# A cross-attention layer and a recurrent layer on one core: work regrouped into two-head units, with new orders for all engines

## The reference

```python
q  = layer_norm((x   + pos_enc).T, ln_q_g,  ln_q_b)        # 256 x 128
kv = layer_norm((ctx + pos_enc).T, ln_kv_g, ln_kv_b)
Q, K, V = split(q @ Wq), split(kv @ Wk), split(kv @ Wv)    # 16 heads of 8
ctx = softmax(Q @ K.T / sqrt(8)) @ V
r   = ctx @ Wo + q
out = gelu(layer_norm(r) @ W1 + b1) @ W2 + b2 + r
x   = out.T                                                # 128 x 256
```

```python
xn = _ln(x); sx = previous row of xn - xn
xxx = tanh((xn + sx * maa_x) @ maa_w1)                     # 5 groups of 32
x5 = xn + sx * (maa_stack + xxx @ maa_w2)                  # 5 mixed inputs
w = exp(-exp(time_decay + tanh(x5[1] @ decay_w1) @ decay_w2))
r, k, v, g = x5[3] @ Wr.T, x5[0] @ Wk.T, x5[2] @ Wv.T, silu(x5[4] @ Wg.T)
for t in range(128):                                       # per head, s is 8 x 8
    a = k_t (outer) v_t;  out_t = r_t @ (u * a + s);  s = a + w_t * s
att = group norm of out over the 8 values of a head
x = x + (att * g) @ Wo.T;  xn2 = _ln(x);  sx2 = previous row - xn2
x = x + sigmoid((xn2 + sx2 * ffn_maa_r) @ Wr.T) * (square(relu((xn2 + sx2 * ffn_maa_k) @ Wk.T)) @ Wv.T)
```

## Time and profile before

| | |
|---|---|
| median of 3 runs | 512.01 us (505.37 to 515.03) |
| span of the profiled execution | 508.9 us; its own time is not given apart, and the runs put it some 3 us above the span |
| PE busy | 393.7 us (77%) |
| DVE busy | 296.2 us (58%) |
| ACT busy | 216.9 us (43%) |
| POOL busy | 149.4 us (29%) |
| mean granted TensorE clock | 0.826 of 2.4 GHz |

### The profile page before, as it was taken

One profiled execution on the slowest core, in us unless ns is written; L12 is line 12 of the kernel. 1 busy time (PEld: TensorE's weight loads), 2 busy tenths in 40 slices (PEclk: granted clock), 3 DMA queues, 4 the chain that ended last, 5 costly groups with the idle time before them and its releaser, 6 DMA issues.

```text
span 508.9 us, 6721 instructions
## 1 busy us (share of the span) xinstructions
PE 393.7 (77%) x2512; PEld 266.0 (52%) x2512; DVE 296.2 (58%) x626; ACT 216.9 (43%) x473; POOL 149.4 (29%) x102
## 2 busy tenths in 40 slices
PE   2437668769887998799989888998997996684624
PEld 0402323526564677367756756675666565563613
DVE  1134144246565967497859776966776455754622
ACT  1201433553564367336735763475446546115001
POOL 4100100110444053415241722263025407235240
PEclk9999999857975899589859986987798689779556
DMA  8340240050314032303421150305030003003000
GB/s 265 144 92 1 64 81 3 20 125 1 95 52 94 6 91 73 83 12 86 117 39 52 44 135 1 95 3 135 1 95 11 2 12 82 11 1 93 10 1 11
DMA packets 35953, 29.74 MB, mean 58 GB/s; under 512 B 3536, under 2 KB 33616, under 8 KB 35792
## 3 DMA queue, kind: packets, MB, share of 16 engines
q1 hardware_dynamic: 35776, 25.86, 20.9%
q10 hardware_dynamic: 144, 3.45, 1.7%
HBM read 20.78 MB, written 8.39 MB: 57 GB/s over the span
## 4 chain that ended last, share of the span: by engine, by line
PE 39%; issue 19%; DVE 15%; POOL 10%; DMA 8%; SPq 4%; ACT 4%; POOLq 0%; ACTq 0%
DMA k_stack<-stacks 6%; POOL v_rep L764 5%; DVE top L808 4%; PE o_bank L363 4%; PE r_one L369 4%; PE h_sum L446 3%; PE r_two L501 3%; PE a_even L412 3%; PE o_bank L550 3%; PE r_one L356 2%; PE r_two L369 2%; PE a_odd L389 2%; PE h_even L434 2%; SPq L308 2%; DVE st L902 2%
## 5 line engine op out<-in xcount | busy, mean ns | idle before, releaser
L808 DVE TENSOR_REDUCE top<-a_even 128x2 f32<-128x512 f32 x64 | 44.1, 688 | 46.9 <-PE a_even L412 33.4
L626 ACT ACTIVATE probs<-h_even 128x512 f32<-128x512 f32 x64 | 38.4, 599 | 57.2 <-PE h_even L434 34.6
L412 PE MATMUL a_even<-k_stack,q_stack 48*128 48x256 bf16 x128 | 32.0, 341 | 31.5 <-DMA k_stack<-stacks 26.8
L771 POOL TENSOR_TENSOR hrs<-hvar,mhalf 128x32 f32<-128x32 f32 x8 | 44.4, 5546 | 37.0 <-DVE hvar L928 37.0
L808 DVE TENSOR_REDUCE top<-a_odd 128x2 f32<-128x512 f32 x64 | 43.6, 682 | 12.9 <-PE a_odd L412 12.9
L902 DVE TENSOR_TENSOR_SCAN st<-dec_rep,v_rep 128x1024 f32<-128x1024 f32 x16 | 40.4, 2528 | 11.6 <-ACT dec_rep L697 5.8
L626 ACT ACTIVATE probs<-h_odd 128x512 f32<-128x512 f32 x64 | 38.6, 603 | 18.5 <-PE h_odd L434 17.7
L446 PE MATMUL h_sum<-probs,v_pad 128*32 128x256 f32 x512 | 43.2, 468 | 0.0
L764 POOL TENSOR_TENSOR v_rep<-v_rep,rk 128x1016 f32<-128x1016 f32 x16 | 39.8, 2485 | 0.0
L434 PE MATMUL h_even<-q_stack,k_stack 50*128 50x256 bf16 x128 | 32.6, 346 | 5.8 <-ACT probs L626 5.3
L412 PEld LDWEIGHTS a_even<-k_stack,q_stack 48*128 48x128 bf16 x128 | 7.7, 101 | 54.1 <-DMA k_stack<-stacks 30.5
(11 more groups left out here) (159 smaller groups left out, 825.2 us busy)
## 6 DMA issues: line engine op xcount, KB each, us to landing
...
W<-in_weights ACTq DMA_DIRECT2D x1, 3368.0 KB, 11.1
stacks<-parts SPq DMA_DIRECT2D x16, 192.0 KB, 2.4
q_stack<-stacks SPq DMA_DIRECT2D x16, 192.0 KB, 3.5
k_stack<-stacks SPq DMA_DIRECT2D x16, 192.0 KB, 4.5
...
```

Of the source, the lines that this page charges most:

```text
L412: mm = pe.matmul(a_score[head % 2][:, j * T:(j + 1) * T], q_stack[g.p][e:e + SCORE_ROWS, head // 2, j * 128:(j + 1) * 128], k_stack[g.p][e ...
L626: act.activation(flat(probs[turn % PROBS][:, :, :]), h_score[HEAD_ORDER[turn] % 2][:, :], ACT.Exp, scale=SCORE_SCALE).then_inc(s_probs, 1)
L771: pool.tensor_tensor(hrs[:, :], hvar[:, :], mhalf[:, :], ALU.pow).then_inc(s_hrs, 1)
L808: dve.tensor_reduce(top[:, :, head], a_score[head % 2][:, :].rearrange("p (a t) -> p a t", a=2), AX.X, ALU.max).then_inc(s_top, 1)
```

## The change

`AT` and `PERIOD` give way to `ORDER`, one written list of operations for each engine (`top.3.5` is part 5 of item 3), no longer periodic. The parts:

- **Two-head units.** `top`, `scores` and `probs` work on a unit of two heads, 8 per item, in one of two PSUM pairs of two banks each (`pairs`), which both kinds share in turn. A reduction or exponential covers 1024 columns.
- **Direct stacks.** The three parts go straight from SBUF into the stacks by 12 DMAs per item, without DRAM.
- **Shared banks.** The other four banks (`banks`) serve all other stretches of all items; `BANKS` says which, and PE waits for the previous user (`wait_bank`).
- **Layer norms in token layout.** `centre` also transposes, so that VectorE adds the centred position code (`dev`), reduces the squares (`ssa`), and multiplies (`nrm`); four transposes (`back`) return it. `var`, `spread`, `h_var`, `h_spread` and POOL's `zsum` go.
- **Mixing.** `maa_stack` becomes a row of the matmul; three products and three sums of up to 512 columns replace L871 and L880, all on VectorE.
- **State.** It is split by value columns, four per scan. Both products by r (`rst`) are on VectorE; `kv` stays on POOL. `read` is 8 matmuls with a constant stationary side of 32 columns and 256 moving columns. The u term is a POOL product (`rkp`), two matmuls and a product (`bon`).
- **Group norm.** Centring moves into a matmul (`cturn`), the squares to ACT, leaving four VectorE operations.
- **First operation of VectorE.** `spread_u` scales a constant of the large weight block and waits for it.

```diff
--- before.py
+++ after.py
...
-        "var_a": 1541, "nrm": 1586, "left": 1645, "parts": 1720,
...
+        "spread_u.0 dev.0 dev.1 var_a.0 var_a.1 nrm.0 dev.2 nrm.1 dev.3 var_a.2 left.0 var_a.3 nrm.2 parts.0 dev.4 var_a.4 "
...
+BANKS = {
+    "dev": "01200030", "nt": "32201011", "qk": "11220111", "v": "33211322", "guard": "10103121", "sum": "30022010",
...
+OPENS = {"centre": "dev", "back": "nt", "qk": "qk", "v": "v", "guard": "guard", "sums.0": "sum", "turn_sums": "sums_t", "turn_ctx": "ctx_t",
...
+        pairs = [stack.enter_context(nc.psum_tensor(f"pair{p}", [128, 4, T], F32)) for p in range(2)]
+        banks = [stack.enter_context(nc.psum_tensor(f"bank{p}", [128, 512], F32)) for p in range(4)]
...
+        def bank(stretch, n):
+            return banks[int(BANKS[stretch][n])]
...
+        def wait_bank(pe, stretch, n):
...
+            if before[stretch, n]:
+                last, m = before[stretch, n]
+                pe.wait_ge(closes[last], m * 3 + thirds[last] if last in thirds else m + 1)
...
-                if a := due(at, "SP", "stack"):
...
-                        sp.wait_ge(s_score_t, (a.n - 1) * H0)
-                    sp.wait_ge(s_spilled[a.p], dma(a, 6))
-                    for side, dst in enumerate((q_stack, k_stack)):
-                        for e in range(2):
-                            sp.dma_start(dst[a.p][64 * e:64 * e + SCORE_ROWS, :, :],
-                                         stacks[a.p, side].rearrange("(i e d) r t -> e (d r) i t", e=2, d=D0)[e]).then_inc(s_stacked[a.p], 16)
...
+                    for side, (tile, which) in enumerate(((q_stack, Q_ROWS), (k_stack, K_ROWS))):
+                        for row in which[part]:
+                            sp.dma_start(tile[p][row::8, :, :], parts[p][:, part, side, :]).then_inc(s_stacked[p], 16)
...
-                if a := due(at, "PE", "var"):
-                    pe.wait_ge(s_dev, a.n * 2 + 2)
-                    for j in range(4):
-                        mm = pe.matmul(a_odd[:, j:j + 1], devsq[:, j // 2, (j % 2) * 128:(j % 2) * 128 + 128], w("mean"),
...
+                p = n % 2
+                if op == "centre":
+                    wait_bank(pe, "dev", n)
+                    pe.wait_ge(s_x_in[p], dma(n, 2))
+                    for side in range(2):
+                        for j in range(2):
+                            mm = pe.matmul(bank("dev", n)[:, (side * 2 + j) * 128:(side * 2 + j + 1) * 128], xin[p][:, side, j * 128:(j + 1) * 128],
+                                           w("center"), start=True, stop=True)
+                    mm.then_inc(s_centred, 1)
+                if op == "back":
...
+                    wait_bank(pe, "nt", n)
...
+                if op == "top":
+                    wait_pair(pe, (op, n, part))
...
                     for j in range(2):
...
+                        for e in range(2):
+                            mm = pe.matmul(pair(op, n, part)[:, 2 * e + j, :], q_stack[p][64 * e:64 * e + TOP_ROWS, part, j * 128:(j + 1) * 128],
+                                           k_stack[p][64 * e:64 * e + TOP_ROWS, part, :], start=True, stop=True)
+                    mm.then_inc(s_scored, 1)
...
-                    if o := due(at, "PE", "read", half):
-                        pe.wait_ge((s_rst_low, s_rst_high)[half], o.n + 1)
-                        for d in range(S1):
-                            mm = pe.matmul(o_bank[:, (half * S1 + d) * 16:(half * S1 + d + 1) * 16], st[:, half, d, :], w("heads"),
-                                           start=True, stop=True)
-                        if half == 1:
-                            mm.then_inc(s_att, 1)
...
+                if op == "read":
+                    wait_bank(pe, "read", n)
+                    pe.wait_ge(s_rst, n * 2 + 2)
+                    for second, name in enumerate(("heads_a", "heads_b")):
+                        for quad in range(4):
+                            mm = pe.matmul(bank("read", n)[quad * QUAD:(quad + 1) * QUAD, 0:E], w(name), flat(st[:, 2 * quad + second, :, :]),
+                                           start=second == 0, stop=second == 1)
+                    mm.then_inc(s_read, 1)
+                if op == "cturn":
...
-                if r := due(at, "POOL", "rst_low"):
-                    pool.wait_ge(s_st, r.n * 2 + 1)
-                    pool.tensor_tensor(st[:, 0, :, :], st[:, 0, :, :], rk[r.p][:, 0, 0, None, :].broadcast_to([128, S1, NT]), ALU.mult).then_inc(s_rst_low, 1)
...
+                if op == "dev":
+                    dve.wait_ge(s_centred, n + 1)
...
+                    dve.tensor_tensor(dev[p][:, :, :, :], bank("dev", n)[:, :].rearrange("p (s j c) -> p s j c", s=2, j=2),
+                                      pe_c[:, None, :, :].broadcast_to([128, 2, 2, 128]), ALU.add).then_inc(s_dev, 1)
+                if op == "var_a":
+                    dve.wait_ge(s_sqa, n + 1)
+                    dve.tensor_reduce(ssa[p][:, :], sqa[:, :, :], AX.X, ALU.add).then_inc(s_ssa, 1)
...
+                if op == "top":
+                    dve.wait_ge(s_scored, n * UNITS + part + 1)
+                    dve.tensor_reduce(top[p][:, :, :, part].rearrange("p j e -> p e j"), pair("top", n, part)[:, :, :].rearrange("p (e j) t -> p e j t", e=2), AX.X, ALU.max).then_inc(s_top, 1)
...
-                        for group in ((0, 1), (2, 3), (4,))[part]:
-                            src = (r_one, r_two, r_one)[part]
-                            for half in range(2):
-                                col = (group % 2) * 256 + half * 128 if group < 4 else half * 128
-                                ins = dve.scalar_tensor_tensor(out=mixed[:, group, half, :], in0=src[:, col:col + 128], scalar=v(f"stack{group}_{half}"),
-                                                               in1=sx[:, half, :], op0=ALU.add, op1=ALU.mult)
...
-                if r := due(at, "DVE", "ruk"):
...
-                        ins = dve.scalar_tensor_tensor(out=ruk[r.p][:, half, :], in0=rk[r.p][:, 0, half, :], scalar=v(f"faaaa_{half}"),
-                                                       in1=rk[r.p][:, 1, half, :], op0=ALU.mult, op1=ALU.mult)
...
+                    dve.tensor_tensor(mixed[p][:, 2 * part:2 * part + count, :, :],
+                                      bank(("m2a", "m2b", "m2c")[part], n)[:, 0:count * E].rearrange("p (k h t) -> p k h t", k=count, h=2),
+                                      sx[p][:, None, :, :].broadcast_to([128, count, 2, NT]), ALU.mult).then_inc(s_mix, 1)
+                if op == "mixed":
+                    dve.wait_ge(s_mix, n * 3 + part + 1)
+                    groups = slice(2 * part, 2 * part + len(MIX_GROUPS[part]))
+                    dve.tensor_tensor(mixed[p][:, groups, :, :], mixed[p][:, groups, :, :],
+                                      xt[p][:, None, :, 1:NT + 1].broadcast_to([128, len(MIX_GROUPS[part]), 2, NT]), ALU.add
+                                      ).then_inc((s_mixed0, s_mixed1, s_mixed2)[part], 1)
...
+                    dve.tensor_tensor_scan(line(st[:, states, :, :]), line(decay[p][:, :, :, :]), line(v_rep[p][:, states, :, :]),
+                                           0.0, ALU.mult, ALU.add).then_inc(s_st, 1)
+                if op == "rst":
+                    dve.wait_ge(s_st, n * 2 + part + 1)
+                    states = slice(4 * part, 4 * part + 4)
+                    dve.tensor_tensor(st[:, states, :, :], st[:, states, :, :], rk[p][:, 0, None, :, :].broadcast_to([128, 4, 2, NT]), ALU.mult
+                                      ).then_inc(s_rst, 1)
...
+                    dve.scalar_tensor_tensor(out=yo[p][:, :], in0=y[:, :], scalar=0.5, in1=x2[p][:, :], op0=ALU.mult, op1=ALU.add).then_inc(s_done, 1)
+                if op == "spread_u":
+                    dve.wait_ge(s_weights, 16)
+                    for half in range(2):
+                        dve.tensor_scalar(spread_u[:, half, :], w("spread"), v(f"faaaa_{half}"), None, ALU.mult).then_inc(s_spread_u, 1)
...
```

1388 lines of the change are left out of this document (734 added, 654 removed), and 88 rows, old and new, of tables (BANKS, ORDER).

## The result

The changed kernel takes **383.44 us** in the median of four runs (381.46 to 384.74), against 512.92 us for the kernel before beside it (four runs, 505.37 to 515.03). The forecast was 373 us, with a range of 338 to 440.

What follows compares the result with a forecast made beforehand. PE, with VectorE next, was taken to set the period, and the two to be level after the change. Start 35, middle 306 and tail 29 gave a 370 us span, 373 us as median; range 338 to 440.

Steps and rivals of the forecast that it cites:

- PE per item: PE's matmul work for one item: from 45.1 to 34.4 us, or 40.2 if pairs save nothing.
- keep their columns: Centring, projections, mixing matmuls and feed-forwards on PE: same columns as before, so a change of 0.
- VectorE per item: VectorE's work for one item: from 37.3 to 35.8 us, including 2.0 us of waiting on GpSimd.
- The alternative beside it: VectorE: by the skill's contention rule, two-SBUF-input operations are exposed and kv blocks fully, total some 27 us higher.
- The start: Up to the first top: VectorE queued behind spread_u's wait for the weight block until 17.4 us; first top at 35.
- The middle: Between first top and tail: PE 253 and VectorE 257 us, level; at 84% full, 306 us.
- from there six items are ready or nearly so: After the first top: VectorE and PE would have work without a gap.
- The tail: From the last read to the end: read 1.9 us, 28.0 following, group norm 0.8 shorter; 29 us.
- Stalls: Fixed lists and shared PSUM banks delay several items: VectorE at 65%, middle 395, total 462 (401 to 502); chance 0.25.
- The list fits well: Engine lists 94% full or more, or VectorE and GpSimd hardly excluding each other: 340 us or less; chance 0.10.
- The lower clock: PE's granted clock stays at 1.2 GHz with less work and more waiting: 527 us in all; chance 0.05.
- The words are not what is done: kv stays on GpSimd; VectorE waiting 4.8 us per item would give 400 us, inside the forecast; no separate chance.

Runs made afterwards that it cites:

- e6: Changed kernel with both heads of each top and scores unit read from the same half of the array's rows; 401.41 us.
- e8: Changed kernel with both kv products and their column copies moved from GpSimd to VectorE, each ahead of its scan; 380.81 us.
- e1: Changed kernel with spread_u moved in VectorE's list from its head to just before item 0's first maximum; 380.56 us.
- e5: Changed kernel with spread_u late and the large weight block issued only after item 0's first exponential; 375.83 us.
- e2: As e1, with the k_stack DMAs of items 0 and 1 issued by ScalarE's queue instead of SP's; 380.53 us.
- e12: Changed kernel with the edits of e5 and e8, plus the k_stack DMAs of items 0 and 1 on ScalarE's queue; 373.22 us.
- e7: Changed kernel with the three mixing sums per item on GpSimd in place of VectorE; 401.1 us.
- e9: Changed kernel with the lower product of the state by r (rst, part 0) on GpSimd, the upper staying on VectorE; 405.05 us.
- e4: Changed kernel with read in its earlier form, sixteen matmuls of 128 by 16 instead of eight of 32 by 256; 413.30 us.

## Why the prediction was right, point by point

- **PE per item**: 34.4 forecast, 36.2 in the run (289.6 / 8). That the middle still agrees to 2 us (253 and 254.6) is partly luck, for two errors cancel: PE's whole work was 289.6 us instead of 275, but 35.0 of it lay in the start and the tail, where 22 was taken off. `read` hit (1.3, 1.27). `top` and `scores` were better than forecast (6.6 for 7.6): the overlap that the prediction took from one pair of the earlier trace rows is real, and worth 36 us of PE (e6). What was dearer is in part the start: centring (L479) takes about 2 us for each of the first four items and 1.1 from 80 us on, as one item had in the period before (L378, 1.1), so the prediction's "keep their columns" holds in the dense stretch and not ahead of it. The rest wasn't traced.
- **VectorE per item**: 35.8 forecast, 36.1 in the run. The 2.0 us carried over for waiting on GpSimd measured 1.9 to 2.3 (e8). It was a choice between 0 and 4.8, so the near hit is partly luck. The alternative beside it, that all instructions with two SBUF inputs are exposed and the sum is 27 us higher, did not come: most of the instructions stretched are these, but only when a product runs at the same time, and that is 1.9 us per item.
- **The start**: 35 forecast, 37.0 came. The step "`spread_u` waits for the weight block, everything on VectorE is queued behind it" was true and incomplete. The same block held PE by way of `xin` (e1, e5): with the first wait gone the first `top` came 2 us earlier, with both gone 8.8. Both waits end at 17.1, so the sum did not suffer.
- **The middle**: 306 forecast at 84%, 316 came at 81%. The step that failed is "from there six items are ready or nearly so, and VectorE and PE have work without a gap". From 37 to 80 us VectorE is 61% busy, afterwards 85%. At 85% these 26.4 us of work would take 31: 12 us lost, the whole difference. The 84% itself was a choice between two rows that lie 17 points apart; that the dense stretch has 85% fits it, but no reading of the old profile gave it, and the hole behind the first maxima was not in it. SP's issues were priced at 0.4 us by a row of another form; the strided ones take 0.6 to 0.65. But a second queue for items 0 and 1 brought nothing (e2, e12), so theirs are not the cause. The rows behind this point show two waits of VectorE that fill the loss, 9.98 us for item 0's transposed sums and 5.41 for the first `top` of item 2. SP's queue issues item 2's stacks only from 63.93, behind `guard.1` in its list, and the last at 71.18. But PE's `top` of item 2 starts at 74.04 without idle time of PE before it, so what held it last was PE's own list, in which it stands behind item 1's scores and sums. With the start 9 us earlier (e5) the two waits were 10.17 and 5.41. That the order of these lists makes them is read, not tested. Timeline of the changed kernel, VectorE:

```profile
68.25 0.36 DVE L1005 RECIPROCAL rden<-bank 128x32 f32<-128x32 f32 x1 [9.98 <-PE bank L551]
...
74.47 2.36 DVE L989 TENSOR_REDUCE top<-pair 128x4 f32<-128x1024 f32 x2 [5.41 <-PE pair L510]
```

PE, and SP's queue:

```profile
74.04 0.90 PE L510 MATMUL pair<-k_stack,q_stack 62*128 62x256 bf16 x8
...
62.37 1.04 SPq L423 DMA_DIRECT2D q_stack<-guard_t  x2
63.93 1.86 SPq L419 DMA_DIRECT2D q_stack<-parts  x3
```

- **The tail**: 29 forecast, 28.4 came, and 28.40 again in e5. The last `read` takes 1.94 us (1.9 forecast), so 26.5 us remain for the rest, where 27.2 was forecast.
- **The rivals.** *Stalls* would have needed 65% in the middle; it had 81. *The list fits well* is not excluded by much: with e5's and e8's edits together the time was 372, still well above 340. *The lower clock* did not come: the mean rose from 0.826 to 0.905. In the stretch from 37 to 80 us it was 0.70, with PE busy for 74% of it. *The words are not what is done* is true (`kv` stays on GpSimd) and is worth at most a few us (e8).
- **The title of the change**, that the state products and mixing sums are on VectorE: in these lists, moving the sums back costs 18 us (e7) and half of the products 22 (e9). `read`'s form gives 30 (e4), the row halves 18 (e6). These are prices around the changed kernel, each alone, and are not to be added up to the 129 us of the whole.
